# Mixture-of-experts tail of a decoder layer: single tiles of 128 rows regrouped into pairs of one expert

## The reference

```
gate_logits = xs @ Wg                                   # 2048 tokens, 8 experts
weights, sel = top_k(gate_logits, 2); weights = softmax(weights)
h     = relu(einsum('td,edf->etf', xs, W1) + b1)        # D = 256, FF = 1024
out_e = einsum('etf,efd->etd', h, W2) + b2
x     = x + sum over the two chosen experts of weight * out_e
```

## Time and profile before

| | us |
|---|---|
| median of 3 runs | 620.53 (619.76 to 622.02) |
| profiled execution, its own time | 621.11 |
| its span, first to last instruction | 619.4 |

### The profile page before, as it was taken

How to read it: one execution, slowest core, us unless ns; L and a number is a source line. 1 busy time by engine, 2 the same in 40 slices (tenths; PEclk the granted TensorE clock), 3 DMA queues, 4 the chain that set the end, 5 groups by cost and what they waited for, 6 DMA issues and landing times.

```text
span 619.4 us, 16540 instructions
## 1 busy us (share of the span) xinstructions
PE 559.7 (90%) x5587; PEld 487.3 (79%) x5588; DVE 357.6 (58%) x841; ACT 329.8 (53%) x726; POOL 232.5 (38%) x301
## 2 busy tenths in 40 slices
PE   3867989999999999878976899999999999999991
PEld 2755767777777777545655899999999999999991
DVE  3547777878686867777458685664223323333231
ACT  4543367665756566414634934565565565665650
POOL 7423122323232412001427253426546555555432
PEclk9878999999999999976975989999999999999996
DMA  8584843444527180840558756657767757766731
GB/s 235 129 119 107 83 71 54 81 77 64 93 52 106 34 125 7 135 139 22 156 170 273 230 152 171 172 170 213 214 174 209 211 173 204 217 174 215 205 91 22
DMA packets 56172, 85.90 MB, mean 139 GB/s; under 512 B 6704, under 2 KB 44880, under 8 KB 56112
## 3 DMA queue, kind: packets, MB, share of 16 engines
q1 hardware_dynamic: 46368, 73.59, 47.2%
q0 software_dynamic: 7872, 10.33, 8.9%
q10 hardware_dynamic: 1872, 1.18, 0.7%
HBM read 62.44 MB, written 9.31 MB: 116 GB/s over the span
## 4 chain that ended last, share of the span: by engine, by line
PE 44%; DMA 28%; DVE 10%; issue 7%; ACT 6%; POOLq 1%; ACTq 1%; POOL 1%; DVEq 0%
DMA out<-y,scatter_now 26%; PE bank L1224 16%; PE pair L2361 4%; PE bank L1610 4%; PE pair L1471 4%; PE pair L1575 4%; DVE row_max L1518 2%; PE bank L2401 2%; PE pair L1506 2%; PE bank L1185 2%; PE bank L1705 1%; ACT hid L2371 1%; ACT prob L1394 1%; ACT p_hi L1397 1%; DMA slots_in<-xn_rows,gather_now 1%
## 5 line engine op out<-in xcount | busy, mean ns | idle before, releaser
L2361 PE MATMUL pair<-slots_t,w_now 128*128 128x128 f32 x1248 | 149.9, 280 | 0.0
L2361 PEld LDWEIGHTS pair<-slots_t,w_now 128*128 128x128 f32 x1248 | 146.6, 197 | 0.1
L2371 ACT ACTIVATE hid<-pair,b_tile 128x128 f32<-128x128 f32 x312 | 88.9, 368 | 56.9 <-PE pair L2361 55.4
L2381 DVE TENSOR_TENSOR hid_lo<-hid,hid_hi 128x1024 fp32r<-128x1024 f32 x39 | 47.8, 1226 | 109.1 <-ACT hid_hi L2378 100.3
L2314 POOL DMA_INDIRECT out<-y,scatter_now x39 | 64.5, 1653 | 117.0 <-DMA out<-y,scatter_now 73.3
L1518 DVE TENSOR_REDUCE row_max<-pair 128x4 f32<-128x1024 f32 x64 | 78.0, 1221 | 18.6 <-PE pair L1506 18.5
L2401 PE MATMUL bank<-experts_w,hid_hi 128*128 x624 | 82.5, 284 | 0.0
L1592 ACT ACTIVATE exp_ring<-pair 128x1024 f32<-128x1024 f32 x64 | 64.8, 1026 | 23.7 <-PE pair L1575 20.9
L2401 PEld LDWEIGHTS bank<-experts_w,hid_hi 128*128 128x128 f32 x624 | 75.7, 188 | 0.0
L2299 POOL DMA_INDIRECT slots_in<-xn_rows,gather_now x39 | 42.3, 1086 | 25.9 <-POOL gather_now L2296 15.2
L2378 ACT ACTIVATE hid_hi<-hid 128x512 fp32r<-128x512 f32 x78 | 49.3, 631 | 4.7
(11 more groups left out here) (293 smaller groups left out, 1042.9 us busy)
## 6 DMA issues: line engine op xcount, KB each, us to landing
w_now<-L_ffn_W SPq DMA_DIRECT2D x39, 1024.0 KB
experts_w<-L_ffn_W SPq DMA_DIRECT2D x8, 1024.0 KB, 8.0
k_stack<-ck_hi SPq DMA_DIRECT2D x32, 128.0 KB, 4.2
q_stack<-cq_hi SPq DMA_DIRECT2D x32, 128.0 KB, 4.3
ctx_in<-ctx SPq DMA_DIRECT2D x8, 256.0 KB, 2.7
k_stack<-ck_lo SPq DMA_DIRECT2D x16, 128.0 KB, 5.2
q_stack<-cq_lo SPq DMA_DIRECT2D x16, 128.0 KB, 5.2
out<-x SPq DMA_DIRECT2D x7, 256.0 KB, 5.0
```

What stands on the lines that cost most here:

```text
L2361: mm = eng.matmul(banks[half][:, f * P:(f + 1) * P], core.w1_now[b.p][:, c, start:start + P], core.slots_t[b.p][:, c, :], start=c == 0, st ...
L2371: act = eng.activation(core.hid[:, g, :], banks[half][:, f * P:(f + 1) * P], ACT.Relu, bias=core.b1_tile[b.p][:, g:g + 1])
L2381: core.m["hid_lo"].at(eng.tensor_tensor(core.hid_lo[b.p][:, :, :], core.hid[:, :, :], core.hid_hi[b.p][:, :, :].bitcast(F32), ALU.subtract))
```

## The change

The first 13 tiles and 8 more (`SINGLES` = 21) stay as they are. The other 18 become 9 pairs (`PAIR_SLOTS`), each pair two tiles of one expert; `last_tiles` gives every expert as many pairs as it has, up to 9 in all, and the tiles left over are the 8 singles. For a pair

- W1 is loaded once, in two halves of 512 columns (2 KB per row of each, 512 KB), all into the one buffer `w1_now[1]`. The load of a half waits for the hidden product of the same half of the pair before. ACT rounds the half to fp32r into `w1_hi` (which lies where `w1_now[0]` was) and DVE writes the rest over the load (`w1_lo`).
- The rows of both tiles are turned into one PSUM bank; ACT rounds them to `x_hi` (256 columns), DVE takes the rest `x_lo`. There is one buffer of each, where each single tile had one of two `slots_t`.
- The hidden product of a half is 24 fp32r matmuls of 256 columns: for each of 4 blocks hi*hi, lo*hi and hi*lo over two halves of D. The relus take 256 columns at once, two per quarter.
- The output of a half is again 24 matmuls, 12 for each tile of the pair; the two outputs of a pair are finished one after the other in its second half.
- POOL gathers pair q+3 between the scatters of pair q, into four buffers used in turn.
- All steps are written out; the loop is gone.
- `first_tiles` and `last_tiles` get more instructions and waits between them.

The core of the diff (the same semaphores are also renamed from `core.w2` to `core.split`):

```diff
-LAST = MAX_TILES + 1 - FIRST
+LAST = MAX_TILES - FIRST
+ODD = NE
+SINGLES = FIRST + ODD
+PAIR_SLOTS = (LAST - ODD + 1) // 2
+assert SINGLES + 2 * PAIR_SLOTS == MAX_TILES
...
-            pipeline(eng, MAX_TILES, MOE_LAG, lambda it: experts(core, name, eng, it), first=UNROLLED)
+            EXPERTS[name](core, eng)
...
+    core.x_hi = sb("x_hi", [KT, 2 * P], F32R)
...
+    core.w1_lo = sb("w1_lo", [KT, FF], F32R)
...
+    core.w1_hi = sb("w1_hi", [KT, FF], F32R)
...
+    core.x_lo = sb("x_lo", [KT, 2 * P], F32R)
...
+    link(core, name, e.tensor_tensor(core.alone[:, :], core.own_tiles[:, :], core.taken[:, :], ALU.subtract))
+    settle(core, name, e)
+    link(core, name, e.scalar_tensor_tensor(out=core.cmp_count[:, :, 0:NE], in0=bc(core.alone[:, :], [P, NE, NE], 2),
+                                      scalar=0.5, in1=bc(core.iota_f[:, 1:NE + 1], [P, NE, NE], 1),
+                                      op0=ALU.mult, op1=ALU.is_ge))
+    settle(core, name, e)
+    link(core, name, e.tensor_reduce(core.tiles_of[0][:, :], core.cmp_count[:, :, 0:NE], AX.X, ALU.add))
+    settle(core, name, e)
     ends = running_sum(core, name, e, [b[:, :] for b in core.tiles_of], NE)
...
+    ends = running_sum(core, name, e, [b[:, :] for b in core.tiles_of], NE)
+    for part, upto, first, done in ((slice(0, ODD), ends, core.singles_at, core.own_tiles),
+                                    (slice(ODD, LAST), core.pairs_to, core.taken, core.singles_at)):
+        n = part.stop - part.start
+        link(core, name, e.tensor_tensor(core.jump[:, 0:NE - 1], first[:, 1:], done[:, 0:NE - 1], ALU.subtract))
+        settle(core, name, e)
+        link(core, name, e.tensor_scalar(core.jump[:, 0:NE - 1], core.jump[:, 0:NE - 1], float(LOCAL[1]), None, ALU.add))
+        settle(core, name, e)
+        tile_numbers(core, name, e, upto, part, NE)
+        link(core, name, e.scalar_tensor_tensor(out=core.col_f[:, part], in0=core.col_f[:, part], scalar=first[:, 0:1],
+                                          in1=core.iota_f[:, 0:n], op0=ALU.add, op1=ALU.add))
+        settle(core, name, e)
     link(core, name, e.tensor_scalar(core.col_f[:, :], core.col_f[:, :], float(COLS[1]), None, ALU.min))
...
+def experts_gpsimd(core, eng):
+    singles(core, "gpsimd", eng, range(SINGLES))
+    for j in range(2):
+        pair_gather(core, eng, 0, j)
+    singles(core, "gpsimd", eng, [SINGLES])
+    for j in range(2):
+        pair_gather(core, eng, 1, j)
+    singles(core, "gpsimd", eng, [SINGLES + 1])
+    for j in range(2):
+        pair_gather(core, eng, 2, j)
+        singles(core, "gpsimd", eng, [SINGLES + 2 + j])
+    for q in range(PAIR_SLOTS):
+        for j in range(2):
+            if q + 3 < PAIR_SLOTS:
+                pair_gather(core, eng, q + 3, j)
+            ex_scatter(core, "gpsimd", eng, unit(q, j))
...
+def experts_tensor(core, eng):
+    singles(core, "tensor", eng, range(SINGLES + 1))
+    last_single(core, "tensor", eng, ex_hidden)
+    pair_rows_tensor(core, eng, 0)
+    ex_out(core, "tensor", eng, tile(SINGLES - 2))
+    for q in range(PAIR_SLOTS):
+        pair_hidden_tensor(core, eng, q, 0)
+        if q == 0:
+            last_single(core, "tensor", eng, ex_out)
+        else:
+            pair_out_tensor(core, eng, q - 1, 1)
+        pair_hidden_tensor(core, eng, q, 1)
+        if q + 1 < PAIR_SLOTS:
+            pair_rows_tensor(core, eng, q + 1)
+        pair_out_tensor(core, eng, q, 0)
+    pair_out_tensor(core, eng, PAIR_SLOTS - 1, 1)
...
+def experts_scalar(core, eng):
+    singles(core, "scalar", eng, range(SINGLES + 1))
+    last_single(core, "scalar", eng, ex_hidden)
+    pair_rows_scalar(core, eng, 0)
+    pair_round_scalar(core, eng, 0, 0)
+    for q in range(PAIR_SLOTS):
+        pair_round_scalar(core, eng, q, 1)
+        pair_relu_scalar(core, eng, q, 0, 0)
+        pair_high_scalar(core, eng, q, 0, 0)
+        pair_relu_scalar(core, eng, q, 0, 1)
+        pair_high_scalar(core, eng, q, 0, 1)
+        if q + 1 < PAIR_SLOTS:
+            pair_round_scalar(core, eng, q + 1, 0)
+        pair_relu_scalar(core, eng, q, 1, 0)
+        pair_high_scalar(core, eng, q, 1, 0)
+        pair_relu_scalar(core, eng, q, 1, 1)
+        if q + 1 < PAIR_SLOTS:
+            pair_rows_scalar(core, eng, q + 1)
+        pair_high_scalar(core, eng, q, 1, 1)
...
+def experts_vector(core, eng):
+    singles(core, "vector", eng, range(SINGLES + 1))
+    last_single(core, "vector", eng, ex_hidden)
+    pair_bias_vector(core, eng, 0)
+    pair_rows_vector(core, eng, 0)
+    pair_rest_vector(core, eng, 0, 0)
+    ex_out(core, "vector", eng, tile(SINGLES - 2))
+    for q in range(PAIR_SLOTS):
+        pair_rest_vector(core, eng, q, 1)
+        pair_low_vector(core, eng, q, 0)
+        if q == 0:
+            last_single(core, "vector", eng, ex_out)
+        else:
+            pair_out_vector(core, eng, q - 1)
+        if q + 1 < PAIR_SLOTS:
+            pair_bias_vector(core, eng, q + 1)
+            pair_rest_vector(core, eng, q + 1, 0)
+            pair_rows_vector(core, eng, q + 1)
+        pair_low_vector(core, eng, q, 1)
+    pair_out_vector(core, eng, PAIR_SLOTS - 1)
...
+def pair_load(core, eng, q, half):
+    core.m["hid"].wait(eng, unit(q, half).back(2))
+    x = pair_expert(core, eng, q)
+    rows = core.t["L0_ffn_W1"].rearrange("e (k p) n -> p e k n", p=P)
+    cols = half_columns(half)
+    core.w1_in.at(eng.dma_start(core.w1_now[1][:, :, cols].rearrange("p (e k) n -> p e k n", e=1),
+                                rows[:, bass.ds(x * -1 + (NE - 1), 1), :, cols]), unit(q, half))
...
+def pair_buffer(core, q, j):
+    n = j if q % 2 else 2 + j
+    return core.slots_in[n], core.gather_now[n]
...
+def pair_gather(core, eng, q, j):
+    b = unit(q, j)
+    rows, now = pair_buffer(core, q, j)
+    core.rows_in.wait(eng, b.back(2))
+    if q == 1:
+        core.m["xT"].wait(eng, tile(SINGLES - 1))
+    elif q > 1:
+        core.m["xT"].wait(eng, pair_step(q - 2))
+    g, col = column_of(core, eng, b)
+    core.m["gnow"].at(eng.tensor_copy(now[:, :], core.gather_idx[g][:, bass.ds(col, 1)]))
+    core.m["gnow"].wait(eng, b)
+    core.rows_in.at(eng.indirect_dma_start(
+        rows[:, :], None, core.xn_dram[0:PARTS[g].stop * P, :],
+        bass.IndirectOffsetOnAxis(ap=now[:, :], axis=0)), b)
...
+def pair_rows_scalar(core, eng, q):
+    core.m["xT"].wait(eng, pair_step(q))
+    core.m["hid"].wait(eng, unit(q, 0).back(1))
+    core.m["slots_t"].at(eng.activation(core.x_hi[:, :, :], core.psum[0][:, :], ACT.Copy))
...
+def pair_round_scalar(core, eng, q, half):
+    core.w1_in.wait(eng, unit(q, half))
+    if q == 0:
+        core.m["hid"].wait(eng, tile(SINGLES - 1), half)
+    else:
+        core.m["hid"].wait(eng, unit(q - 1, half))
+    cols = half_columns(half)
+    eng.activation(core.w1_hi[:, :, cols], core.w1_now[1][:, :, cols], ACT.Copy).then_inc(core.split["hi"], 1)
...
+def pair_hidden_tensor(core, eng, q, half):
+    u = unit(q, half)
+    bank = core.pair[u.p]
+    if half == 0:
+        core.m["slots_t"].wait(eng, pair_step(q))
+    eng.wait_ge(core.split["hi"], NE + 2 * q + half + 1)
+    for f in range(UNIT):
+        if f % 2 == 0:
+            core.m["h"].wait(eng, u.back(2), f // 2)
+        col = (half * UNIT + f) * P
+        out, cols = bank[:, f * 2 * P:(f + 1) * 2 * P], slice(col, col + P)
+        products(eng, out, [(core.w1_hi[:, k, cols], core.x_hi[:, k, :]) for k in range(KT)], start=True)
+        if f == 0:
+            eng.wait_ge(core.split["lo"], NE + 2 * q + half + 1)
+        products(eng, out, [(core.w1_lo[:, k, cols], core.x_hi[:, k, :]) for k in range(KT)])
+        if f == 0 and half == 0:
+            eng.wait_ge(core.x_rest, q + 1)
+        mm = products(eng, out, [(core.w1_hi[:, k, cols], core.x_lo[:, k, :]) for k in range(KT)], stop=True)
+        if f % 2 == 1:
+            core.m["hid"].at(mm)
...
+def pair_out_tensor(core, eng, q, half):
+    u, x = unit(q, half), pair_expert(core, eng, q)
+    hi, lo = (unit_rows(w[u.p][:, :, :]) for w in (core.hid_hi, core.hid_lo))
+    core.m["hid_hi"].wait(eng, u)
+    for j in range(2):
+        b = unit(q, j)
+        ps = core.psum[1 + b.p]
+        if half == 0:
+            core.m["y"].wait(eng, b.back(2), 0)
+        for term, (left, part) in enumerate(((hi, 0), (hi, 1), (lo, 0))):
+            if term == 2 and j == 0:
+                core.m["hid_lo"].wait(eng, u)
+            for f in range(UNIT):
+                at = part * FT * D + (half * UNIT + f) * D
+                mm = eng.matmul(ps[:, 0:D], left[:, f, j * P:(j + 1) * P],
+                                core.experts_w[:, bass.ds(x * PLACE + at, D)],
+                                start=half == 0 and term == 0 and f == 0,
+                                stop=half == 1 and term == 2 and f == UNIT - 1, skip_group_check=True)
+        if half == 1:
+            core.m["out"].at(mm)
```

(63 more changed lines are left out.)

104 lines of the change are left out of this document (73 added, 31 removed).

## The result

The changed kernel takes 623.17 us in the median of 20 runs, the kernel before 620.37 in 20 runs beside them: ratio 1.0045, 95% interval [1.0025, 1.0066]. That is +2.8 us where -2.5 was forecast. It lies within the range given and just within the 0.5% that I called "same", but on the other side of zero, and the interval leaves zero out. The profiled execution took 619.98 us, its span is 618.1; before, the profiled one took 621.11 with a span of 619.4. So the profiled execution of the changed kernel lies 3.2 us under the median of its runs and that of before 0.7 over its own, and the two traces differ by -1.3 us where the medians differ by +2.8. The medians are of all runs, the ratios leave out the few that took over 1.5% longer than the fastest of their kernel.

A forecast was written before the change was run, and what follows sets the result against it. PE was taken to set the pace, with the chained scatters close behind. Terms -10.8 + 2.2 + 4.2 + 0.2 + 1.7 = -2.5 us took the median from 620.5 to 618.0 us, range 614.8 to 623.5.

The forecast's parts named there:

- the routing tables: Longer `last_tiles` on DVE delays the gather of tile 13 to 423.2, wanted at 425.55: 0 taken, up to 1.6 us.
- PE's work in a pair: Matmuls and transposes of a pair take 12.00 us instead of 13.20 for two tiles: -10.8 us over nine pairs.
- The ring: Reloading W1's one buffer by halves: a load has 4.0 us, takes 3.5, so it is hidden with half a microsecond left.
- The rival (0.11): W1's half load takes 5.6 us, 1.6 late, so a pair takes 13.6 us: 629 us in all, chance 0.11.
- DVE's order: DVE's steps in a pair end near S + 12.2, PE wants the last at S + 12.5: hidden, 0.3 us left.
- Scatters in the pairs: Two scatters per pair, taken as 5 us each, are hidden up to a cycle of 6.0 us.
- Start of the pairs: The first half of W1 cannot be rounded before tile 20, the last single, is through: +2.2 us (0 to 3).
- The end: After the last matmul, the last scatter comes 8.2 us later where it was 3.9: +4.2 us (2 to 6).
- No loop: Written-out code fetches its instructions by DMA; with small handovers: +1.7 us (0 to 6).
- Gathers: In the pairs, gathers run three pairs ahead and nothing waits for them: 0.
- `first_tiles`, +0.2: Two more waits of at most 0.18 us each on the way to the first gather: +0.2 us (0 to 0.4).

The follow-up runs named there:

- y_first: The changed kernel with VectorE doing the output step of tile 8 ahead of the second routing list: 617.33 us, 0.9963; a second time 618.62 us, 0.9945.
- after_again: The changed kernel measured again with no edit, against the kernel before on the same chip: 622.47 us, ratio 1.003.
- after_gather: The changed kernel, with SyncE's load of W1 for tile 13 also waiting for the gather of tile 13: 616.88 us, ratio 0.9943.
- before_late5: The kernel before, with five unused running sums (about 4.0 us of VectorE) ahead of `last_tiles`: 628.43 us, ratio 1.0108.
- y_first_ring: y_first, with each half load of W1 from the second pair on also waiting for the relus of the product that freed its half: 643.82 us, 1.0372.
- y_first_end: y_first, with VectorE in the last pair doing both output steps of pair 7 ahead of the rest of hid: 619.78 us, ratio 0.9968.
- y_first_twin: y_first, with the scatter of a pair's second tile not waiting for that of its first: 611.99 us, ratio 0.9882.
- before_unrolled: The kernel before with all 39 tiles written out and no loop: 620.13 us, ratio 1.0006.

## Why the prediction was wrong

**The step that failed** is the one on the routing tables: "A scatter of as many bytes takes 3.7 to 3.9 from its issue, and that adds to what stands in DRAM, a gather only reads: 0 taken (up to 1.6)". It measured +7.3 in the trace; in the medians taking the hole away is worth 5 to 6 us (`y_first` against `after_again` -5.1, +2.8 against -3.0 for `after_gather`). The direction was seen and the sum was close as far as DVE; reckoned from the hidden product of tile 11, I had the gather issued at +4.0 (423.2 - 419.16) and wanted at +6.4. It went at +5.3, 0.5 later because the tables took 8.15 us, not 7.7, and because DVE's list slid with them, and 0.8 later because the scatter ahead of it held POOL 2.43 us, not the usual 1.6. Then it took 5.7 us to land. Three things were missing in the bound:
- The load. After tile 11's hidden product SP issues 1 MB at once; before, the gather was out 3.7 us ahead of it (419.99 against 423.73), now it came 0.75 us behind. I priced the gather alone, although the prediction says elsewhere that traffic behind 1 MB loads is slow. `after_gather` shows this part: 5.70 against 3.07.
- The clock. A stop of 4.5 us did not only cost 4.5: the product behind it ran at half clock and took 2.4 more. `before_late5` shows the same in the old kernel, 6.13 us behind a stop of 4.26; stops of 0.5 to 1.8 us at this place show none of it.
- The bound itself. The gather had 2.3 us to land, the nearest row said 3.7 to 3.9, and I argued that row away. With it the step would have been +1.5, with the 5.70 measured here +3.4, and the clock's 2.4 on top.

**The other steps.**
- PE's work in a pair, -10.8: right. Half a product takes 2.83 us and a pair 11.94 on the mean (half 1 of the first pair starts at 496.84, of the ninth at 592.40), forecast 2.89 and 12.0: 9 x (11.94 - 13.20) = -11.3. Two tiles' products now take 5.66 us in three fp32r terms where they took 6.98 in float32, and that 1.3 us is the whole gain of a pair.
- The ring: right in kind, in size partly by luck. A half load lands in 3.9 by the page (3.5 to 5.6), 3.5 was taken, 4.0 allowed, which would leave 0.1; no stop for it in the pairs, and 0.6 us in hand by `y_first_ring`. So the allowance was too small by about as much as the load was priced too low. The rival (0.11) stood nearer than its chance said.
- DVE's order: nearly right. It is hidden with 0.2 us left in some pairs, where 0.3 was forecast, and in five it is late, 1.0 us in all.
- Scatters in the pairs, 0: right, PE never stands for one there.
- Start of the pairs, +2.2: 1.1 us of waiting for `w_lo`, and the first product starts 0.4 us later than eight tiles at 6.60 would have it (489.76 - 436.60 = 53.16 against 52.8): 1.5 in all.
- The end, +4.2: +4.4 by size, but for another reason. Not DVE's order sets when the last four scatters start, but the scatter before them (`y_first_end`); what removes them is running two at once (`y_first_twin`).
- No loop, +1.7: nothing that shows by `before_unrolled`, interval -1.7 to +2.4 us. Mis-sized: more fetched instructions were visible in the queue, and nothing waited for them.
- Gathers, 0: right for three ahead, and the reason given ("nothing waits for them") hid that at two ahead everything would. `first_tiles`, +0.2: not measured by itself.

With the measured sizes and no hole the sum is -11.3 + 1.5 + 4.4 = -5.4, beside -5.5 found above; the hole adds 7.3 and gives +1.9, beside +1.8 measured from tile 11 on in the two traces. The medians say +2.8, the whole spans -1.3; that difference is not explained. `y_first` and `after_gather` come to -2.3, -3.4 and -3.5 us by their ratios, less than 5.4. A part is in the pairs, whose thin covers do not hold in every trace: from the product that waits for `w_lo` to the last matmul PE takes 109.6 us in the changed kernel, 110.5 and 111.1 in the two measurements of `y_first`, 113.8 in `after_gather`, where it stands for `x_hi` up to 0.58 us before a pair. Their profiled spans (614.7, 614.1, 617.1) lie 2.3 to 5.3 under that of before, so another part is the spread of the runs. What sets either was not followed.

## What to carry to other kernels

When a change lengthens work on an engine that is idle two thirds of the time, follow the queue behind it to the next transfer, and look at what that transfer will now stand behind: a gather that slips past the issue of a large load pays for the load as well. Price a stop of PE of several us with the slow matmuls that follow it, and look for a reordering first, since here one moved statement or one wait was worth 5 to 6 us, more than the whole change brought even with it. Where transfers are chained only because two of them might touch the same rows, a regrouping that makes them disjoint is worth using for that as well.
